# A planner's rule for late steps in the first batch, with a shorter horizon and earlier dates for the second feed-forwards

## The reference

```python
x = x + 0.5 * ffn(layernorm(x), W_r, W_k, W_v, mu_r, mu_k)      # first feed-forward
x = x + attention(layernorm(x), W_qkv, b_qkv, W_proj, b_proj)   # 16 heads of 16, rope, causal
x = x + 0.5 * ffn(layernorm(x), W_r, W_k, W_v, mu_r, mu_k)      # second feed-forward, same weights
# ffn(x): x_prev is x moved by one row of time; xr, xk mix x and x_prev by mu_r, mu_k;
#         out = sigmoid(xr W_r') * (relu(xk W_k')^2 W_v')
```

## Time and profile before

| | |
|---|---|
| time, median of 3 runs | 3033.27 us (3032.0 to 3041.44) |
| profiled execution, its time | 3033.34 us |
| its span | 3031.6 us |
| PE busy | 2899.2 us (96%) |
| DVE busy | 2454.8 us (81%) |
| ACT busy | 2191.8 us (72%) |
| POOL busy | 1581.5 us (52%) |

### The profile page before, as it was taken

One profiled execution on the slowest core, in us unless ns is written; L12 is line 12 of the kernel. 1 busy time (PEld: TensorE's weight loads), 2 busy tenths in 40 slices (PEclk: granted clock), 3 DMA queues, 4 the chain that ended last, 5 costly groups with the idle time before them and its releaser, 6 DMA issues.

```text
span 3031.6 us, 56206 instructions
## 1 busy us (share of the span) xinstructions
PE 2899.2 (96%) x18245; PEld 1712.0 (56%) x18245; DVE 2454.8 (81%) x7302; ACT 2191.8 (72%) x4802; POOL 1581.5 (52%) x2190
## 2 busy tenths in 40 slices
PE   6797999999999999999999999999999999999997
PEld 4444555555656555555655655565565655565344
DVE  3885888888888888888888888888888888888862
ACT  4475777777777777777777777777777777777663
POOL 5454455555555555555655555555555555554322
PEclk9898999999999999999999999999999999999998
DMA  3424354344434434434433534443443543443411
GB/s 101 79 51 71 68 99 78 76 89 82 94 70 103 82 68 96 79 86 86 89 82 69 109 63 98 85 81 82 76 106 63 102 79 76 88 82 85 83 47 36
DMA packets 202585, 245.49 MB, mean 81 GB/s; under 512 B 68405, under 2 KB 104245, under 8 KB 202293
## 3 DMA queue, kind: packets, MB, share of 16 engines
q1 hardware_dynamic: 202293, 241.90, 39.1%
HBM read 53.48 MB, written 51.38 MB: 35 GB/s over the span
## 4 chain that ended last, share of the span: by engine, by line
PE 77%; DVE 13%; ACT 4%; issue 3%; POOL 1%; DMA 1%; SPq 1%; POOLq 0%; DVEq 0%; ACTq 0%
PE ps_y L977 17%; PE ps_s L946 14%; PE ps_m L956 13%; PE ps_d L1030 7%; PE ps_d L1033 7%; PE ps_d L1042 6%; PE ps_d L1036 6%; DVE ps_m L1183 4%; PE ps_d L1046 3%; DVE mx_sb L1186 3%; PE ps_d L1023 2%; ACT pt_sb L1072 2%; PE ps_d L984 2%; DVE ka_sb L1208 1%; DVE qb_sb L1241 1%
## 5 line engine op out<-in xcount | busy, mean ns | idle before, releaser
L1072 ACT ACTIVATE pt_sb<-ps_s 128x512 f32<-128x512 f32 (+1 forms) x2532 | 1221.4, 493 | 458.4 <-PE ps_s L946 431.2
L1183 DVE CUSTOM_DVE_ANT_0 ps_m<-ps_m,mask_sb 128x128 f32<-128x128 f32 (+3 forms) x2048 | 996.8, 497 | 332.7 <-PE ps_m L956 314.6
L956 PE MATMUL ps_m<-kr_sb,qr_sb 96*128 96x512 bf16 (+3 forms) x3072 | 1000.0, 329 | 52.9 <-DVE mx_sb L1183 17.6
L946 PE MATMUL ps_s<-qr_sb,kr_sb 99*128 99x512 bf16 (+1 forms) x3039 | 993.0, 329 | 30.9 <-ACT pt_sb L1072 20.7
L1186 DVE TENSOR_REDUCE mx_sb<-ps_m 128x1 f32<-128x512 f32 x1024 | 698.6, 682 | 96.4 <-PE ps_m L956 88.7
L1315 POOL TENSOR_SCALAR_AFFINE_SELECT pt_sb<-pt_sb 128x512 f32<-128x512 f32 x384 | 256.8, 669 | 531.7 <-ACT pt_sb L1072 529.0
L956 PEld LDWEIGHTS ps_m<-kr_sb,qr_sb 96*128 96x128 bf16 x3072 | 301.8, 98 | 372.9 <-DVE mx_sb L1183 51.6
L977 PE MATMUL ps_y<-pt_sb,v_sb 128*32 128x512 f32 (+2 forms) x5120 | 492.7, 493 | 3.8 <-POOL pt_sb L1315 3.5
L946 PEld LDWEIGHTS ps_s<-qr_sb,kr_sb 99*128 99x128 bf16 x3039 | 292.8, 96 | 330.8 <-issue 132.1
L1072 ACT ACTIVATE pn_sb<-ps_s 128x384 f32<-128x384 f32 x507 | 246.6, 492 | 216.2 <-PE ps_s L946 214.6
L1042 PE MATMUL ps_d<-axn_sb,wqk_sb 128*128 128x256 f32 x1024 | 312.7, 391 | 5.2 <-ACT axn_sb L1112 3.8
(11 more groups left out here) (113 smaller groups left out, 3891.5 us busy)
## 6 DMA issues: line engine op xcount, KB each, us to landing
kr_sb<-part_sb SPq DMA_DIRECT2D x378, 128.0 KB, 4.5
qr_sb<-part_sb SPq DMA_DIRECT2D x378, 128.0 KB, 4.8
y_way<-yt_sb SPq DMA_DIRECT2D x128, 256.0 KB, 2.3
sw_sb<-qb_sb SPq DMA_DIRECT2D x496, 64.0 KB, 2.0
x_sb<-x SPq DMA_DIRECT2D x64, 256.0 KB, 3.9
yn_sb<-y_way SPq DMA_DIRECT2D x64, 256.0 KB
den_sb<-r_way SPq DMA_DIRECT2D x64, 256.0 KB
out<-x_sb SPq DMA_DIRECT2D x64, 256.0 KB, 2.6
```

The source lines that it names most:

```text
L946: eng.matmul(score_bank(slot)[:, 0:width], kr_sb[0:KR + NP, n % RS, j, kb * P:(kb + 1) * P], qr_sb[0:KR + NP, n % RS, j, q0:q0 + width], s ...
L956: eng.matmul(ps_m[:, u % NM, 0:width], qr_sb[0:KR, n % RS, j, i * P:(i + 1) * P], kr_sb[0:KR, n % RS, j, piece * QC:piece * QC + width], s ...
L1072: eng.activation(buffer[:, j, column:column + width], score_bank(slot)[:, 0:width], ACT.Exp, scale=SCALE).then_inc(exped, 1)
L1183: eng.tensor_tensor_reduce(ps_m[:, u % NM, 0:width], ps_m[:, u % NM, 0:width], mask_sb[:, m0:m0 + width], 1.0, -3e38, ALU.add, ALU.max, be ...
```

## The change

It does three things, all in the planner; no instruction is added or taken away.

- The horizon EARLY goes from 60 to 50: a dense step may stand at most 50 slots ahead of its date (never before slot 48, if its date is later than slot 64).
- A second feed-forward of batches 0 to 13 has a date 20 slots sooner. With the shorter horizon its earliest slot is 10 slots sooner; that of all other steps with a late enough date is 10 slots later.
- In slots below 192 a dense step of ACT, DVE, POOL or SP that is more than five slots past its date is placed as soon as its inputs are ready, without the test for room.

```diff
-    EARLY_HEAD, EARLY = 16, 60
+    EARLY_HEAD, EARLY = 16, 50
+    LATE = 5
@@ def release
-            return at + BSLOTS + 70 + 24 * c
+            return at + BSLOTS + 50 + 24 * c
@@ def pick
-            if early > slot or not self.ready(now - self.margin(e, slot), after) or e != "PE" and rank[0] == 2 and self.TAKES[name][0] + self.shut(name, now) > room:
+            if early > slot or not self.ready(now - self.margin(e, slot), after) or e != "PE" and rank[0] == 2 and not self.overdue(rank, slot) and self.TAKES[name][0] + self.shut(name, now) > room:
                 continue
@@
+    def overdue(self, rank, slot):
+
+        return slot < BSLOTS and rank[1] < slot - self.LATE
```

## The result

The changed kernel is a little slower, by 0.7%: 3056.81 us in the median (3053.37 to 3059.84) against 3034.98 for the kernel before, measured beside it (3032.0 to 3041.44). The ratio is 1.0066, with a 95% interval of 1.0049 to 1.0084. I had forecast 3018.

The account below looks back on a forecast made before the run. PE's work was taken to bound the long middle, with one 16 us PE wait in batch 0. From the median, 3033.3 - 16.1 - 2.3 + 3 = 3017.9, about 3018 us; range for 8 in 10: 3003 to 3034.

Parts of the forecast that it names:

- The wait of batch 0 goes: At slot 127, PE's one 16.14 us wait for batch 1's rows of q and k was to vanish whole: -16.1 us.
- the half-speed piece: Right after that wait PE runs 4.6 us at the 1.2 GHz level; this was to go too: -2.3 us.
- rival B: Batch 0 also loses its other idle time (6.8 to 1.6) and the half-speed piece at 183.0 us: 3006 us; chance 0.15.
- Standing steps cost 3 us of 0 to 12.3: Before slot 192, late steps placed ahead of maxima on DVE delay reductions PE waits for: 0 to 12.3 us, taken as 3.
- The collision: A two-input DVE step and a POOL step reading SBUF take turns: r_sin took 1.70 us beside r_cos, against 1.08 mean.
- The middle: 0 a batch: Later batches: sooner second feed-forwards move only PE's 2.1 us idle time a batch; bounds -2.1 to +4.3, taken as 0.
- The prediction's sign for it: A batch of the middle taking 180.5 us or more would show the middle getting slower.
- Rival D: The middle gets slower, 2.2 us in each of 13 batches: 3047 us; chance 0.12.
- D's reason: With horizon 50 and feed-forwards moved against ropes, PE finds no ready dense step at one more place in every batch.
- The tail: 0: The last two batches keep their dates, so no change was expected there: 0 us.

## Why the prediction was wrong, by its own steps

- *The wait of batch 0 goes, -16.1, and the half-speed piece, -2.3*: right. The gaps in the chain closed (f_k0 and f_k1 now run together from 173.1 us), the row copies land in time, and PE's clock is 1.00 from slot 127 on. The earlier half-speed piece, at 183.0 to 189.8 us, is gone too, as rival B had it, but another has come at 233 us, after PE had waited for maxima and for ACT in the 20 us before, 2.5 at the longest:

```profile
231.20:241.20 10.00, 9.48 (x34) 4.73 (x34) 7.92 (x28) 6.60 (x17) 6.70 (x11) 0.66 0.70 125
```

- *Standing steps cost 3 us of 0 to 12.3*: the sum for slots 48 to 192 was 140.5 us and they took 144.5, so the cost there was 7. The collision that I had weighed as a rule against the change was there at once: f_k0 and f_k1 of chunk 7 took 2.90 us together, beside POOL steps that follow one another without a gap from 171.3 us on, and PE waited 1.5 for them. The test for room that the rule waives also counts `shut`, the time until POOL is free by the planner's clock, for f_k, f_r, r_sin and r_add; the sum didn't reckon with losing that. Batch 1 then gave 5.3 us back (176.0 instead of 181.3), which the sum didn't have. Start as a whole: 16.7 gained, 15.4 forecast.
- *The middle: 0 a batch*: this is the step that failed. It was +3.0 in each of 12 batches (I had counted 13; batch 14 is short), inside the bounds of -2.1 and +4.3. I took 0 because the dates were spread as before. What the runs show in its place is new waits of PE, 31 us over the twelve batches, for f_k0 and f_k1 and for masked maxima. The prediction's sign for it, a batch of 180.5 us or more, came with 182.3. The row that should have weighed more was the 2.1 us of idle time a batch: an order with so little left to win has more room to get worse. Rival D named the mechanism of the loss (a new wait of PE in every batch) and priced it at 2.2 a batch, with a break-even of 1.2; it was given 0.12.
- *D's reason* was only half right. PE doesn't lack ready dense steps: f_K has its written place, and f_k is late; or the bank of a maximum isn't free. The reason stood in the prediction, but at the start and not at the middle: r_sin took 1.70 us beside r_cos. The Trainium skill, SBUF — State Buffer, "Who interferes with whom", has the rule. The runs agree with it: in the changed order f_k1 fell beside f_xadd (1.58 against 0.48 us), and with f_xadd and a_bias cut to a quarter it took 0.92 at the most. That nobody waits for such a step in the old order and PE does in the new one, no row of the kernel before could tell.
- *The rival nobody had*: that the planner's order has two repeating kinds, and that each part of the change alone leads into the one with a wait in every batch. The rows showed one of them only. That the change came out at +0.7% and not at +5% was as little to be read from them. A range that allowed for it would have reached past 3200 (the parts alone took 3169 to 3241).
- *The tail: 0*: right for the order. The clock moved it by 5.5 us between the profiles.

## What to carry to other kernels

When a program's order comes from a greedy planner that carries its state from one round into the next, a term can't be priced by "the dates hardly change": compare the written orders of several rounds first, at the one deadline that everything waits for, and try the neighbours of each number. Keep a rule in it that pulls late steps forward in every round, so that a drift is taken back. And a step that is moved on VectorE has to be priced beside the GpSimd step that it will meet, not by its mean.

## What the runs showed of the hardware

An f_k1 with its two inputs in SBUF took 1.58 us beside a POOL sum of 1.27 us that began within 0.02 us of it, against 0.48 alone. Either side can be the one that is lengthened. Where f_k had begun 0.05 us ahead, it kept its 0.48 and f_xadd took 1.55 instead of 1.27; where f_xadd had begun 0.44 us ahead, f_k took 1.49 (f_xadd's own 1.64 began beside an r_sin of DVE, 0.15 us older):

```profile
993.33 0.48 DVE L1213 SCALAR_TENSOR_TENSOR ka_sb<-dif_sb,muk_sb,fxn_sb 128x256 f32<-128x256 f32 x1
...
1010.66 1.49 DVE L1213 SCALAR_TENSOR_TENSOR ka_sb<-dif_sb,muk_sb,fxn_sb 128x256 f32<-128x256 f32 x1
```

```profile
993.38 1.55 POOL L1348 TENSOR_TENSOR x_sb<-x_sb,dif_sb 128x512 f32<-128x512 f32 x1
...
1010.22 1.64 POOL L1348 TENSOR_TENSOR x_sb<-x_sb,dif_sb 128x512 f32<-128x512 f32 x1 [1.67 <-DVE dif_sb L1225]
```

Cutting two kinds of POOL steps (188 instructions of the run) to a quarter of their columns made the changed kernel 79 us faster and the kernel before 29 us, by single runs, though POOL is busy only half of the time and holds 1% of the chain that ended last. And the last 85 to 91 us of the same order differ by about 5 us between runs; the other engines' busy times agree, and PE's granted clock doesn't (0.87 and 0.81).
